# Edge tiles of a GNN kernel: nodes filled to two edges instead of four, iterations of 16 tiles, and one GpSimd wait fewer in each

## The reference, cut to what matters

```python
edge_mats = (bond_features @ W_bond + b_bond).reshape(-1, d, d)
for _ in range(STEPS):                                   # 4
    msg = einsum('eij,ej->ei', edge_mats, h[nbr])        # nbr = dst of the edge
    agg = segment_sum(msg, src_of_edge, n_atoms)
    h = gru_cell(agg, h, W_ih, W_hh, b_ih, b_hh)
x = x + h
h = relu(layernorm(x))
norm = deg_inv_sqrt[row] * edge_weight * deg_inv_sqrt[col]
out = x + segment_sum(h[row] * norm[:, None], col, n_nodes)
```

## Time and profile before

| what | value |
|---|---|
| time before | 32952.45 us (median of 3 runs, 32952.38 to 32958.36) |
| span of the profiled execution | 27350.5 us |
| the profiled execution's time outside its span | not shown by the page; the median is 5601.95 us above the span |
| GpSimd busy | 19773.5 us, 72% of the span |
| gathers of the four steps | 13680, 944 ns busy each |
| scatters of the message stage | 3420, 958 ns busy each |

### The profile page before, as it was taken

How to read it: one execution, slowest core, us unless ns; L and a number is a source line. 1 busy time by engine, 2 the same in 40 slices (tenths; PEclk the granted TensorE clock), 3 DMA queues, 4 the chain that set the end, 5 groups by cost and what they waited for, 6 DMA issues and landing times. The chain is left out here.

```text
span 27350.5 us, 248811 instructions
## 1 busy us (share of the span) xinstructions
PE 12418.6 (45%) x67848; PEld 9414.8 (34%) x67849; DVE 10433.9 (38%) x18392; ACT 4610.5 (17%) x9766; POOL 19773.5 (72%) x20823
## 2 busy tenths in 40 slices
PE   6666664555555455555455555545555530000004
PEld 5444443343433334343343434334343420000004
DVE  9999995333332333323333333233333331111114
ACT  5333332111111111111111111111111110000000
POOL 2777777777777777777677777777777767777772
PEclk6777776777777677777677777767777765555555
DMA  3333332111111111111111111111111112222214
GB/s 107 119 121 119 119 121 63 28 29 29 28 28 27 28 28 28 28 28 28 26 28 28 29 29 28 27 28 28 28 28 28 28 33 51 51 51 51 51 50 139
DMA packets 1844050, 1332.28 MB, mean 49 GB/s; under 512 B 1186181, under 2 KB 1764306, under 8 KB 1824975
## 3 DMA queue, kind: packets, MB, share of 16 engines
q1 hardware_dynamic: 613600, 907.71, 11.2%
q0 software_dynamic: 666016, 352.94, 8.3%
q10 hardware_dynamic: 564300, 70.11, 1.6%
HBM read 986.53 MB, written 342.65 MB: 49 GB/s over the span
## 5 line engine op out<-in xcount | busy, mean ns | idle before, releaser
L1107 POOL DMA_INDIRECT h_rows<-h_table,rec x13680 | 12910.7, 944 | 4241.4 <-issue 4124.3
L1296 PE MATMUL outer<-a_masked,h_by_quarter 128*128 128x136 f32 x27360 | 5300.6, 366 | 8599.6 <-DVE h_by_quarter L1151 8599.6
L1296 PEld LDWEIGHTS outer<-a_masked,h_by_quarter 128*128 128x128 f32 x27360 | 4986.4, 268 | 9066.4 <-issue 9065.7
L1342 ACT COPY outer_sums<-outer 128x408 f32<-128x408 f32 x4560 | 2276.2, 499 | 14771.5 <-PE outer L1296 14269.5
L1151 DVE TENSOR_TENSOR h_by_quarter<-h_rows,gates 128x1920 f32<-128x1920 f32 x912 | 1964.4, 2154 | 6780.7 <-DMA h_rows<-h_table,rec 6780.7
L1591 POOL DMA_INDIRECT messages_by_bucket<-ms,ix x3420 | 3276.8, 958 | 1065.5 <-issue 1033.2
L863 POOL DMA_INDIRECT edges_by_node<-row,place x3125 | 2992.8, 958 | 959.7 <-issue 953.9
L1261 PE MATMUL msg_psum<-outer_sums,w_bond_blocks 128*128 128x480 f32 x7752 | 3471.4, 594 | 0.0
L1144 DVE TENSOR_TENSOR a_masked<-rec,gates 128x2040 f32<-128x2040 f32 x912 | 2074.2, 2275 | 3660.6 <-PE outer L1296 3639.9
L1261 PEld LDWEIGHTS msg_psum<-outer_sums,w_bond_blocks 128*128 128x128 f32 x7752 | 1551.6, 211 | 1373.4 <-issue 1373.4
L1573 PE MATMUL pgb<-ident_f,gsp_by_chunk_of_tile 128*120 128x128 f32 x228 | 61.6, 426 | 3832.2 <-DVE gsp_by_chunk_of_tile L1498 3832.2
(11 more groups left out here) (274 smaller groups left out, 12420.3 us busy)
## 6 DMA issues: line engine op xcount, KB each, us to landing
h_rows<-h_table,rec POOLq DMA_INDIRECT x13680, 2.4
key_row<-source_keys SPq DMA_DIRECT2D x125, 1600.0 KB
rec<-edges_by_node SPq DMA_DIRECT2D x1140, 157.5 KB, 2.4
low_key_row<-source_low_keys SPq DMA_DIRECT2D x126, 800.0 KB
mr<-messages_by_bucket SPq DMA_DIRECT2D x220, 392.0 KB, 3.1
messages_by_bucket<-zeros SPq DMA_DIRECT2D x125, 689.5 KB
carry_flags<-carry_flags SPq DMA_DIRECT2D x285, 240.0 KB
chunk_sums<-scan_t ACTq DMA_DIRECT2D x912, 60.0 KB
```

What stands on the lines that cost most here:

```text
L1107: pool.indirect_dma_start(out=hb[j][:, u, :], out_offset=None, in_=ht, in_offset=bass.IndirectOffsetOnAxis(ap=rec[j][:, u, W_DST:W_DST + 1 ...
L1296: last = pe.matmul(pt[(j * NB + g) % RING][:, at:at + KC], hq[j % 2][:, u, :, :].rearrange("p q d -> p (q d)"), am[j % 2][:, u, :, :].rear ...
L1342: act.copy(ts[b][:, :, at:at + w].rearrange("p k (u c) -> p u k c", c=CPT), pt[(j * NB + g) % RING][:, 0:GPB * KC].rearrange("p (u k c) -> ...
```

## The change

`CH` goes from 4 to 2, so that a node's slots are filled up to an even number: T3 = (400000 + 12500) / 128, rounded up to a multiple of 32, which is 3232. `J3` becomes 16 and `GI` 2, so that a step has 202 iterations in 101 groups. There are 16 chunks instead of 8 in a quarter of a tile, so that an outer product has 272 columns for 136 and a `weigh` product 512 for 480; a group still needs 17 of them. The `weigh` products are now put one behind each lot of outer products, the lots have 2 tiles for 3, and the ring has 2 buffers of two banks. Four sets of buffers stay (`RB`). GpSimd waits for outer products only in front of an iteration's first gather. `JD` becomes 8, so that 99 groups still cover all destinations. The chunk tables double (206848 rows for 109440), and the chunks of a group are stored in `TU` = 4 stores as before.

```diff
-CH = 4
+CH = 2
-J3 = 15
-GI = 4
-DIV15 = 4370
+J3 = 16
+GI = 2
+TU = 4
+RB = 4
-JD = 15
+JD = 8
...
-            GPB = 3
+            GPB = 2
-            RING = 4
-            WEIGH_AT = (NB + 1) // 2
-            HALF = WEIGH_AT * GPB
+            RING = 2
...
                         def group(n0, ng, b, i, g, past):            # GpSimd
                             for j in range(GI):
-                                pool.wait_ge(s_rec[j], ng * 16 + 16)
+                                r = b * GI + j
+                                pool.wait_ge(s_rec[r], (s * USES[b] + i) * 16 + 16)
                                 pool.wait_ge(s_hb, n0 + j + 1)
                                 for u in range(J3):
-                                    if u in (0, HALF) and not (past == 0 and j < 2):
-                                        pool.wait_ge(s_t, n0 * NB + (j * NB + NB + u // GPB))
+                                    if u == 0 and past:
+                                        pool.wait_ge(s_t, n0 * NB + (j * NB + NB))
...
                         def group(n0, ng, b, i, g, past, last=False):   # VectorE
                             if past == 2:
                                 scan(ng - 2, b, s * USES[b] + i - 1)
                                 take_dst(g)
-                            for j in range(GI):
-                                if j + 1 < GI:
-                                    make_a(n0 + j + 1, ng, j + 1, (j + 1) % 2)
-                                if past == 2 and j == 2:
-                                    add_degrees(g)
-                                spread_h(n0 + j, ng, j)
-                                if past == 2 and j == 0:
-                                    onehots_of_dst(g)
+                            spread_h(n0, b, i, 0)
+                            make_a(n0 + 1, b, i, 1)
+                            if past == 2:
+                                onehots_of_dst(g)
+                                add_degrees(g)
+                            spread_h(n0 + 1, b, i, 1)
...
                             for j in range(GI):                          # TensorE
                                 for g in range(NB):
-                                    if g == WEIGH_AT and past:
-                                        weigh(ng - 1, 1 - b, n0 * NB + RING, j)
...
                                     last.then_inc(s_t, 1)
+                                    if past:
+                                        k = j * NB + g
+                                        weigh(ng - 1, 1 - b, n0 * NB + RING, k, k + 1 if k < GI * NB - 1 else K1)
```

252 lines of the change are left out of this document (130 added, 122 removed).

## The result

The changed kernel takes **34250.38 us** (median of four runs, 34239.44 to 34267.53), the kernel before 32952.88 us: 1.0393 times as long, with a 95% interval of 1.0379 to 1.0408. The forecast was 31889 us, faster; it is slower, and outside the range. Its profiled execution took 34267.53 us around a span of 34266.0, so that 1.53 us lie outside the span. Nothing like the 5602 us that the prediction put there fits in.

What follows compares the result with a forecast made beforehand. GpSimd's instruction count at a fixed pace was taken as the bound. Terms -938.5 - 237.4 + 81 + 32 = -1063 us, with 5601.95 us held fixed, took 32952.45 to 31889 us; range 31480 to 32380 us.

Steps and rivals of the forecast that it cites:

- I take them as a fixed amount outside the span: Median minus profiled span: 5601.95 us, taken as lying outside the span and held fixed by the change.
- the wait in front of the tenth gather: GpSimd's mid-iteration wait for outer products: never held it beyond the ordinary gap, so removal is worth nothing.
- rival two: The 5602 us lie in the pace, 0.269 us more per GpSimd instruction; time 31555 us, chance 0.26.
- Fewer tiles: Steps lose 752 gathers, 938.5 us off; message stage loses 188 scatters, 237.4 us off; together 1175.9 us.
- The wait in front of the first gather: GpSimd's wait for outer products each iteration: slack 2.0 us, stall 0.2 us in each of 404 groups, 81 us.
- the copy is done before its buffer is wanted; cost nothing: ScalarE and the two-buffer ring: a lot takes TensorE 1.77 us, a copy about 0.65 us, so no cost.
- The clock: TensorE bursts start at the low level, losing 1.4 to 3.1 us; in the middle about 0.2 us stall a group.
- Rivals one: TensorE's clock rises late in every group, 1.1 us in 404 groups, 444 us; time 32253 us, chance 0.21.
- Rival three: TensorE lacks its high clock in mixed bursts, stalling 12 us a group, 4850 us; time 36660 us, chance 0.08.
- VectorE's order: The first iteration's spread stands behind the scan, delayed if TensorE is late; in the upper end, not the sum.
- A rule weighed: VectorE's two-port lockout of GpSimd would let longer a_masked hold gathers, 1900 us worse; by the rows it does not.
- Seams: After each step's last gather, TensorE's longer burst adds about 8 us in each of four seams, 32 us.

Runs made afterwards that it cites:

- h4: Changed kernel with GpSimd's wait for outer products put back, in front of the ninth gather, for the first four lots of the iteration before; 32371.96 us, 0.9818 of the kernel before.
- e0: Kernel before, unedited, profiled again; ratio 0.9999 to the kernel before, span 33160.2 us.
- e2: Kernel before with GpSimd waiting for outer products only in front of an iteration's first gather, not the tenth; ratio 1.0031 to the kernel before.
- f1: Changed kernel with one gather in each iteration instead of 16, its rows spread for all 16 tiles; 28051.98 us, 0.853 of the kernel before (one run).
- e3: Changed kernel with VectorE's spread of a group's first iteration put ahead of the scan; ratio 1.0266 to the kernel before.
- f4: Changed kernel with the spread ahead of the scan and GpSimd waiting for outer products of iteration n - 3 instead of n - 2; ratio 1.1342 to the kernel before.
- i1: Changed kernel with a 400-column GpSimd memset and a wait behind each gather, slowing gathers to 1.56 us; ratio 1.0094 to the kernel before.

## Why the prediction was wrong

**The failed step is the first one**, "I take them as a fixed amount outside the span". With it fails the term that turned the sign, the wait in front of the tenth gather, put at nothing: 1895 us by h4, as said below. The median was 20% above the span of the trace, and the trace was read as if the timed runs looked like it. They do not: e0 takes the time of the kernel before (ratio 0.9999) with a span of 33160.2 us, and 5679 of the 5810 us more are in the place stage, steps, scatters and seams. The prediction's own rival two had the right place, "in the pace", but spread them evenly over GpSimd's instructions; a gather is still 0.943 us. In the place stage and the steps they stand beside waits for late signals of TensorE, which no row of the first trace holds; in the message stage it is the scatters that are held. The one hint was there: 5602 us of launch is a very odd number. The Trainium skill, Runtime: NRT & Kernel Launch, "The ~15µs preamble/postamble breakdown", gives 9 to 15 us for a launch and was set against this step in the prediction itself. The traces agree that it is no thousands of us: 1.53 us around the span after, less still than the Trainium skill has, and the measurement decides.

**Fewer tiles.** The counts came true, the prices did not. The scatters gave 266 us (4808.7 us for 4543.1, first to last) for 237.4. In the steps a gather is not worth 1.248 us. With lateness mostly kept away as in h4 (0.27 us), a step takes 4823 us for e0's 4953, so the four gain 520 us, not 938.5; e0's own lateness, 2.37 us, is in that comparison.

**The wait in front of the tenth gather**, "its removal is worth nothing". Right by the trace, wrong in the timed runs: putting a like wait back takes 1895 us off the changed kernel (h4), while the kernel before loses only 0.3% without it (e2). It was costed as a wait; it worked as a brake. h4 lies at 0.9818 of before, the way that was forecast; without this wait's removal the sign would have come out right.

**The wait in front of the first gather.** Predicted 2.0 us of slack and 81 us of stalls; measured 3990.7 + 1068.3 us. The pieces were sized well: a lot of four passes is 1.08 us (3 x 0.229 + 0.39), a copy 0.61 us (0.65 said), a_masked 4.68 (4.67), the spread 2.28 (2.29). But the eight lots of a group's first iteration, with the weigh products between them, take 23.5 us in the median from the start of the first pass to that of the last, where the sum said 14.0; without the gathers, in f1, they take 16.7. The sentence "the copy is done before its buffer is wanted; cost nothing" is where the lateness enters. A slip beside it: the terms listed for a group add up to 29.9 us of TensorE, not 30.6; that touches only the pause that was estimated from it.

**The clock.** Rivals one and three feared it; the granted clock of a step rose from 0.74 to 0.83. Rival three had the sign by luck: its price rested on the clock, its 36660 us are too much, and its actual mechanism was not in the text.

**VectorE's order.** The scan in front of the spread did hold the loop: it starts 8.7 us in the median after the last pass of TensorE's last lot begins. e3 took that away and gained 1.2%; a lateness of 2.55 us stayed.

**A rule weighed.** The gathers beside the longer a_masked take 938 to 982 ns, as before; so the measurement stays against such a hold. a_masked is a TENSOR_TENSOR, and no run here shows that it runs in a two-port mode, so it is open whether the rule speaks of it at all.

**Seams.** 8 us more each was said; they are 264 us for e0's 252, so 12.

## What to carry to other kernels

If a profiled span and the timed median differ by more than a launch, take a second trace before any sum: a trace that does not reproduce the time cannot price waits. A wait with no measured idle time may still be what keeps a producer from outrunning a queue; look at what runs freely once it is gone. Where another engine's signals come late beside back-to-back indirect DMAs, try pacing the DMAs, by a wait or by idle work, before adding lead; look first whether their packets are late at all.

## What the runs showed of the hardware that was not expected

Beside back-to-back gathers of 128 rows, in every trace but the first, TensorE's signals arrive late by up to 27.6 us (the most in f4; there the lot that begins at 12029.92 and takes 1.18 is copied at 12054.47), while its passes keep their 0.229 us at the high clock, the gathers' packets land in about 2 us and the signals of VectorE and ScalarE are prompt. They become prompt as the gathers' pace goes from 1.39 to 1.46 us. The Trainium skill, SBUF — State Buffer, "Who interferes with whom", says that a DMA never contends with a compute engine; the passes' pace agrees. The Trainium skill speaks there of the ports of SBUF, so the late signals are no evidence against it.

**Open** is what the signals queue behind, and why the first execution of before was free of it. One difference is visible. The first page gives 2.4 us from issue to landing for the gathers; no later page can, since many records of landings are missing (e0's trace holds 150658, the first 395655; the packets of the transfers are all there in both). The page of e0:

```profile
h_rows<-h_table,rec POOLq DMA_INDIRECT x13680
```

The Trainium skill, NOTIFIC — the notification-queue block, "7.1 Overflow: three behaviours, one of which stalls the engine", describes notification records that, in one of three settings, hold up an engine when their queue is full. The traces give that rival some weight. A gather's landing has 16 records. They are all there, but for 27 of 218880, in the first trace, all there in f1 and 92% there in i1, and these are the three traces with the least lateness (0.14, 0.04 and 0.04 us); in the others 16 to 52% are there. The scatters go at 1.263 us where their records are complete (the first trace) and at 1.404 to 1.410 where 7 to 9% are left. In between the order is not strict: h4 keeps 24% at a lateness of 0.27 us, e0 52% at 2.37. So what fills may be the path of the records and not one that the kernel itself needs; then the 1.4 us, the brake and the value of pacing would hold for executions that are recorded. No run here shows whether that is the cause, nor whether an execution that records nothing has it; every timed run here reports its span and clock as the profiled ones do.
